# First attention of a two-layer sandwich: projections as three products of rounded parts, v for two heads at once

## The reference

```python
qkv = jnp.einsum('bnd,ed->bne', x, w_qkv)          # x: 4 x 512 x 256, w_qkv: 6144 x 256
q, k, v = to_heads(split(qkv, 3))                  # 16 heads of 128
q, k = rope(q, k)
valid = (j > i - 64) & (j <= i)
scores = where(valid, einsum('bhnd,bhkd->bhnk', q, k) / sqrt(128), -inf)
out = einsum('bhnk,bhkd->bhnd', softmax(scores), v)
y = einsum('bni,di->bnd', out, w_o)
```

## Time and profile before

| what | value |
|---|---|
| median of 3 runs | 3217.12 us |
| lowest and highest | 3216.79 and 3224.24 us |
| the profiled execution's own time | 3226.86 us |
| its span in the profile | 3225.1 us |
| TensorE matmul busy | 2566.4 us, 80% |
| VectorE, ScalarE, GpSimd busy | 52%, 38%, 40% |
| mean granted TensorE clock | 0.908 of full speed |
| first attention, first matmul to last | from 61.7 to 757.2 us of the span |

### The profile page before, as it was taken

The page is one execution under the profiler, slowest core; times in us unless marked ns, Lnnn a source line. Parts: engine busy times, 40 slices in busy tenths (PEclk is TensorE's granted clock), DMA queues, the critical chain, the costliest instruction groups (busy, mean ns, idle before and its releaser), DMA issues. The chain is left out here.

```text
span 3225.1 us, 44443 instructions
## 1 busy us (share of the span) xinstructions
PE 2566.4 (80%) x12088; PEld 1642.3 (51%) x12088; DVE 1680.2 (52%) x5549; ACT 1238.9 (38%) x3462; POOL 1297.1 (40%) x1229
## 2 busy tenths in 40 slices
PE   2999999994699899899989959991385575589993
PEld 1777777773354545545544546651232233266662
DVE  3555555555366366266366353336556456653334
ACT  0333333333355255255255334441154452523331
POOL 0333333332255255155255317883302202106885
PEclk9999999997899999999999959995686887879996
DMA  4000000000100000000000064552000000133554
GB/s 134 11 14 13 13 9 13 13 8 0 75 1 1 1 1 1 1 1 1 2 1 1 1 219 82 86 85 62 21 1 0 0 0 0 62 111 67 87 85 108
DMA packets 72708, 112.21 MB, mean 35 GB/s; under 512 B 11649, under 2 KB 59521, under 8 KB 72129
## 3 DMA queue, kind: packets, MB, share of 16 engines
q0 software_dynamic: 30336, 42.73, 8.3%
q1 hardware_dynamic: 37968, 63.15, 5.7%
q10 hardware_dynamic: 4224, 4.19, 0.4%
HBM read 80.69 MB, written 36.32 MB: 36 GB/s over the span
## 5 line engine op out<-in xcount | busy, mean ns | idle before, releaser
L969 POOL TENSOR_TENSOR b_sm<-b_sm,b_rden 128x128 f32<-128x128 f32 (+3 forms) x512 | 368.0, 721 | 286.0 <-DVE b_rden L937 283.9
L879 ACT ACTIVATE b_sm<-b_sm,b_mn 128x128 f32<-128x128 f32 (+3 forms) x512 | 287.2, 561 | 364.5 <-DVE b_mn L931 364.1
L789 PE MATMUL b_s<-b_k,b_q 128*128 128x128 f32 (+3 forms) x688 | 261.2, 465 | 36.8 <-POOL b_q L956 36.8
L366 POOL TENSOR_TENSOR a_q<-a_prod 128x512 f32<-128x512 f32 x64 | 81.5, 1274 | 485.5 <-DVE a_prod L312 485.5
L931 DVE CUSTOM_DVE_ANT_0 b_sm<-b_s,maskB 128x128 f32<-128x128 f32 (+3 forms) x344 | 167.2, 486 | 160.6 <-issue 158.5
L798 PEld LDWEIGHTS b_t<-ident,b_sm 128*128 128x128 f32 x1280 | 162.2, 141 | 169.6 <-issue 117.4
L798 PE MATMUL b_t<-ident,b_sm 128*128 128x128 f32 x1280 | 225.7, 274 | 11.5 <-DVE b_pt L923 4.9
L1337 POOL DMA_INDIRECT XN<-rows,m_slots x158 | 158.1, 1001 | 95.7 <-DVE m_slots L1499 48.2
L810 PE MATMUL b_o<-b_pt,b_v 128*64 128x512 f32 (+3 forms) x1024 | 191.7, 457 | 3.9 <-DVE b_pt L923 3.9
L789 PEld LDWEIGHTS b_s<-b_k,b_q 128*128 128x128 f32 x688 | 106.2, 194 | 137.5 <-DVE b_mn L931 102.5
L321 DVE CUSTOM_DVE_ANT_0 a_s<-p_s,maskA 128x192 f32<-128x192 f32 (+1 forms) x256 | 71.7, 336 | 200.2 <-issue 200.2
(11 more groups left out here) (278 smaller groups left out, 5812.3 us busy)
## 6 DMA issues: line engine op xcount, KB each, us to landing
WM<-in_m_w_dram SPq DMA_DIRECT2D x4, 3072.0 KB, 15.6
WM<-in_m_w_dram SPq DMA_DIRECT2D x4, 2432.0 KB, 12.9
acc<-in_zeros_dram SPq DMA_DIRECT2D x3, 2176.0 KB, 15.8
a_w<-in_a_w_dram SPq DMA_DIRECT2D x16, 384.0 KB, 3.1
n_part<-acc SPq DMA_DIRECT2D x12, 512.0 KB, 7.8
b_w<-in_b_w_dram SPq DMA_DIRECT2D x1, 3072.0 KB, 10.0
XN<-rows,m_slots POOLq DMA_INDIRECT x158
X<-in_x_dram SPq DMA_DIRECT2D x4, 512.0 KB, 3.8
```

Source lines behind the costliest of these rows:

```text
L789: pe.matmul(p_s[g % 3][:, 0:keys(t)], q_r[:, m % 2, t * P:(t + 1) * P], kp[:, m // B_REP % 2, head, 0:keys(t)], start=True, stop=True).the ...
L879: act.activation(sm[:, g % RING, 0:keys(t)], sm[:, g % RING, 0:keys(t)], ACT.Exp, scale=-1.0, bias=mn[:, g % RING:g % RING + 1], accum_out ...
L969: pool.tensor_tensor(sm[:, s, 0:keys(t)], sm[:, s, 0:keys(t)], rden[:, s:s + 1].to_broadcast([P, keys(t)]), ALU.mult).then_inc(s_pn, 1)
```

## The change

The norm stage n0 writes two arrays in place of one: ScalarE copies the turned rows from PSUM into `HTp[0]`, of type fp32r (rounded, the high part), and VectorE subtracts that from the PSUM value into `HTp[1]` (the low part). The weights of a pair of heads arrive in two pieces: piece a (512 KB: q and k of the first head, v of both heads) and piece b (256 KB: q and k of the second head). ScalarE rounds each piece (`high_a`, `high_b`), GpSimd subtracts (`low_a`, `low_b`). Every projection is then three products, high x high, high x low and low x high, of fp32r operands. v is computed only at u = 0 to 3, for both heads at once, in two halves of the same bank with ScalarE's copy between them. The split of piece a for the next pair stands at the end of step u = 5 on ScalarE and GpSimd, that of piece b at the end of step u = 1; for the first pair both stand at the head of the stage. The last pair is written out as the first is.

```diff
@@ attention0, SyncE
-                load_w(0, 0)
-                load_w(1, 1)
+                load_a(0)
+                load_b(0)
                 load_wo(0)
                 with sp.Fori(1, PAIRS) as i:
-                    sp.wait_ge(s_proj, i * (3 * U) - 3 * BATCH)
-                    load_w(i * 2, 0)
-                    sp.wait_ge(s_proj, i * (3 * U))
-                    load_w(i * 2 + 1, 1)
+                    sp.wait_ge(s_lo_a, i)
+                    load_a(i)
+                    sp.wait_ge(s_lo_b, i)
+                    load_b(i)
@@ attention0, TensorE
+                def three(out, lhs, rhs, k):
+                    for n, (a, b) in enumerate(((0, 0), (0, 1), (1, 0))):
+                        mm = pe.matmul(out, lhs(a), rhs(b), start=(k == 0 and n == 0), stop=(k == KD - 1 and n == 2))
+                    return mm
                 def qk(i, u, j, bank):
+                    w = w_a if u < BATCH else w_b
+                    if j == 0 and b == 0:
+                        pe.wait_ge(s_lo_a if u < BATCH else s_lo_b, i + 1)
                     on(pe, s_prod, 2 * n - 1 + j)
                     for k in range(KD):
-                        mm = pe.matmul(bank[:, :], w[:, slot, k, j, :], c.HT[:, k, b * SEQ:(b + 1) * SEQ],
-                                       start=(k == 0), stop=(k == KD - 1))
+                        mm = three(bank[:, :], lambda a: w[:, a, k, j, :], lambda a: c.HTp[a][:, k, b * SEQ:(b + 1) * SEQ], k)
                     mm.then_inc(s_proj, 1)
                 def v(i, u):
-                    on(pe, s_v, n)
-                    for t in range(TB):
-                        for k in range(KD):
-                            mm = pe.matmul(p_v[:, t * P:(t + 1) * P], c.HT[:, k, b * SEQ + t * P:b * SEQ + (t + 1) * P],
-                                           w[:, slot, k, 2, :], start=(k == 0), stop=(k == KD - 1))
-                    mm.then_inc(s_proj, 1)
+                    for half in range(2):
+                        on(pe, s_v, i * U + 2 * b + half)
+                        for t in range(2):
+                            at = b * SEQ + (2 * half + t) * P
+                            for k in range(KD):
+                                mm = three(p_v[:, t * 2 * P:(t + 1) * 2 * P], lambda a: c.HTp[a][:, k, at:at + P],
+                                           lambda a: w_a[:, a, k, 2:4, :], k)
+                        mm.then_inc(s_proj, 1)
@@ attention0, ScalarE
                 def copy_v(i, u):
-                    act.wait_ge(s_proj, 3 * n + 3)
                     on(act, s_ov, n - 3)
-                    act.activation(v_s[:, u % 4, :, :].rearrange("p t n -> p (t n)"), p_v[:, :], ACT.Copy).then_inc(s_v, 1)
+                    for half in range(2):
+                        act.wait_ge(s_proj, projected(i, u) + 3 + half)
+                        act.activation(v_s[:, :, u, 2 * half:2 * half + 2, :],
+                                       p_v[:, :].rearrange("p (t h n) -> p h t n", t=2, h=2), ACT.Copy).then_inc(s_v, 1)
+                def high_a(i):
+                    act.wait_ge(s_wa, i * 16 + 16)
+                    on(act, s_proj, i * (3 * U) - 2 * BATCH)
+                    act.activation(w_a[:, 0, :, :, :], raw_a[:, :, :, :], ACT.Copy).then_inc(s_hi_a, 1)
@@ attention0, GpSimd
                     if alive(i, u, 0):
                         rope(i, u, 1, k_r)
+                    if u == 5 and more(i):
+                        low_a(i + 1)
+                    if u == 1 and alive(i, u, 0) and (not isinstance(i, int) or i > 0):
+                        low_b(i)
+                def low_a(i):
+                    pool.wait_ge(s_hi_a, i + 1)
+                    pool.tensor_tensor(w_a[:, 1, :, :, :], raw_a[:, :, :, :], w_a[:, 0, :, :, :].bitcast(F32),
+                                       ALU.subtract).then_inc(s_lo_a, 1)
@@ sandwich
-                norm_stage(nc, c, "n0", x_dram=x, outs=((c.HT, None, None),))
-                attention0(nc, c, a_w, a_wo)
+                norm_stage(nc, c, "n0", x_dram=x, outs=((c.HTp, None, None),))
+                attention0(nc, c, a_wa, a_wb, a_wo)
```

More of the change, by code:

```diff
@@ L153, in passes @@
                     step(0, u)
-                with eng.Fori(1, PAIRS) as i:
+                with eng.Fori(1, PAIRS - 1) as i:
                     for u in range(U):
                         step(i, u)
+                for u in range(U):
+                    step(PAIRS - 1, u)
                 for u in range(3):
@@ L168, in out_of, with projected, more @@
                 return (u - 3) % U - BATCH if (u - 3) % U >= BATCH else None
+            def projected(i, u):
+                return i * (3 * U) + (4 * u if u < BATCH else 2 * u + 2 * BATCH)
+            def more(i):
+                return not isinstance(i, int) or i + 1 < PAIRS
             def outs_before(i, u):
@@ L222, in values @@
                         width = P if t == TB - 1 else A_SPAN
-                        mm = pe.matmul(p_o[:, t * P:t * P + width], v_s[:, (u - 2) % 4, t, :], pt[:, t, 0:width],
+                        mm = pe.matmul(p_o[:, t * P:t * P + width], v_s[:, slot, b, t, :], pt[:, t, 0:width],
                                        start=(t == 0), stop=(t == TB - 1), skip_group_check=True)
@@ L248, in step @@
                         turn(i, u)
-                    if alive(i, u, 0):
+                    if alive(i, u, 0) and u < BATCH:
                         v(i, u)
@@ L300, in step @@
                         exp(i, u)
+                    if u == 5 and more(i):
+                        high_a(i + 1)
+                    if u == 1 and alive(i, u, 0) and (not isinstance(i, int) or i > 0):
+                        high_b(i)
+                high_a(0)
+                high_b(0)
                 passes(act, step)
@@ L381, in step, with low_b @@
                         rope(i, u, 1, k_r)
+                    if u == 5 and more(i):
+                        low_a(i + 1)
+                    if u == 1 and alive(i, u, 0) and (not isinstance(i, int) or i > 0):
+                        low_b(i)
[3 more added lines that the diff above has]
+                                       ALU.subtract).then_inc(s_lo_a, 1)
+                def low_b(i):
+                    pool.wait_ge(s_hi_b, i + 1)
+                    pool.tensor_tensor(w_b[:, 1, :, :, :], raw_b[:, :, :, :], w_b[:, 0, :, :, :].bitcast(F32),
+                                       ALU.subtract).then_inc(s_lo_b, 1)
+                low_a(0)
+                low_b(0)
                 pool.wait_ge(s_z, 1)
@@ L424, in norm_stage @@
         has_xn = residual and not final
-        split = any(isinstance(o[0], tuple) for o in outs)
+        split = any(isinstance(o[0], list) for o in outs)
         def sems(used, *names):
@@ L632, in _ @@
                 steps = {}
+                if split:
+                    steps[16] = high_part
                 if store is not None:
@@ L2060, in sandwich @@
                 c.maskA = scope.enter_context(nc.sbuf_tensor("maskA", [P, A_SPAN], F32))
+                c.HTp = [scope.enter_context(nc.sbuf_tensor(f"HT_part{i}", [P, KD, TOKENS], F32R)) for i in range(2)]
                 load("constants_a", ((c.ident[:, :], ident), (c.cosA[:, :], a_cos), (c.sinA[:, :], a_sin),
@@ L2175, in layout @@
     d = {"x": i["L0_attn_x"]}
-    d["a_w"] = i["L0_attn_w_qkv"].reshape(3, A_HEADS, A_HD, KD, P).transpose(1, 4, 3, 0, 2)
+    qkv = i["L0_attn_w_qkv"].reshape(3, A_HEADS // 2, 2, A_HD, KD, P).transpose(1, 5, 4, 2, 0, 3)
+    d["a_wa"] = np.concatenate([qkv[:, :, :, 0, 0:2], qkv[:, :, :, :, 2]], 3)
+    d["a_wb"] = qkv[:, :, :, 1, 0:2]
     d["a_wo"] = i["L0_attn_w_o"].T.reshape(A_HEADS, A_HD, DIM)
```

38 lines of the change are left out of this document (23 added, 15 removed).

## The result

| what | before | after |
|---|---|---|
| median of 4 runs | 3218.68 us | 3272.02 us |
| lowest and highest | 3216.79 and 3224.24 us | 3266.41 and 3272.6 us |
| the profiled execution's own time, and its span | 3226.86 and 3225.1 us | 3266.41 and 3264.6 us |
| first q of the first attention | 61.67 us | 67.10 us |
| last sum into Y | 763.27 us | 812.48 us |

The changed kernel is slower: 1.0159 times the kernel before, 95% interval 1.0141 to 1.0177. In the experiments each ratio is to the kernel before as it ran beside them (medians 3218.68 to 3222.23 us), and differences to the changed kernel are to 3272.02 us.

The account below looks back on a forecast made before the run. Long units were taken as bound by TensorE's matmuls, short ones by a chain through VectorE and GpSimd. Stage +15, start +5.4 and clock +30 made +50 us on the 3217.1 median: 3267 us, range 3228 to 3293.

Parts of the forecast that it names:

- stage without clock: Attention stage: unit-length changes summed over all pairs of heads, +2.8 us a typical pair, together +15 us.
- The start: Before the first q: ScalarE's copy +1.25, larger load +0.6, rounding and subtracting 1.06 + 2.43 + 0.05; sum +5.4 us.
- The stall of v: At u = 0 to 3, TensorE waits 0.86 us between v's halves for ScalarE's copy out of the shared bank.
- Unit 6: Rotary sum of q waits behind GpSimd's subtraction of the next weights: delayed 3.1 us, unit 12.1 us, +2.65.
- Unit 7: Without v, the values wait 1.2 us for ScalarE's copies; unit 10.4 us in place of 11.84, -1.44.
- The product: Projections on TensorE: an fp32r product costs 0.213 us for 512 columns (upper end 0.24), 0.112 for 256.
- the dear product: Rival: products cost 0.24 us for 512 columns and 0.13 for 256, +23 us over the stage, 3290 us; chance 0.12.
- The clock: TensorE's clock falls in short units' gaps at two to four places a pair, 4.3 us a pair, +30 us.
- the holding clock: Rival: no gap is idle enough to lower TensorE's clock, leaving +15 + 5.4, 3237 us; chance 0.14.
- the fast product: Rival: products run quicker than their columns at 2.4 GHz, 0.12 us for 512, about 3204 us; chance 0.06.
- the rounded products do what they say: Rival denying this: fp32r products in the projections cost as much as float32, six times 0.86 for q; chance below 0.01.
- the removed v was off it: At u = 4, 5, v lay off the chain, so removing it saves nothing; only q's 0.43 us counts.

Follow-up runs that it names:

- the kernel of the filled gaps: Changed kernel plus unused float32 matmuls of 512 columns in TensorE's gaps at u = 4 to 6; 3250.62 us, 1.0099 times the kernel before.
- the first experiment: Changed kernel with piece a's split at u = 4, both roundings before the exponentials, subtraction after k's rotary sum; 3250.75 us, 1.0086 times the kernel before.

## Why the prediction was right, step by step

The forecast was 3267 us and the measurement 3272.02, on the side forecast. The steps, with the kernel of the filled gaps as the measurement at the full clock:

| step | predicted | measured, full clock | measured |
|---|---|---|---|
| u = 0 to 2 | 12.73 | 13.18 | 13.18 |
| u = 3 | 9.27 | 9.73 | 9.73 |
| u = 4, 5 | 9.04 | 9.13 | 9.13 |
| u = 6 | 12.1 | 11.99 | 13.08 |
| u = 7 | 10.4 | 10.73 | 11.5 |
| a pair | +2.8 | +5.0 | +6.9 |
| start | +5.4 | | +5.4 |
| stage without clock | +15 | +28 | |
| clock | +30 | | +16 |

- **The start.** Its load, rounding and subtraction were put at 4.14 us beyond today's way to the first product and took 4.13, because each had a row of its own shape or near it. That the sum is 5.4 too is luck: the remaining 1.25, for ScalarE's copy, is smaller than what the same code varies by, and the first q of the eight kernels with this start comes 3.8 to 6.1 us later than in the profiled execution before.
- **The stall of v**, 0.86 predicted, is 0.85. Moving the values into it gives back 0.94, since the first product behind a wait costs 0.10 more, which the sum did not have.
- **Unit 6.** The subtraction was to end at S + 6.9, and the rotary sum behind it starts at 6.86; the delay of 3.1 us for a rotary sum that stands behind foreign work was right, and moving that work removes 2.85.
- **Unit 7.** The values wait 1.11 us for the copies that v used to cover, 1.2 predicted.
- **The product was mis-sized.** "I take 0.213, with 0.24 as the upper end": the records show 0.230 for 512 columns, and 0.119 for 256 in place of 0.112. In a long unit that is 0.20 for q and k, 0.17 for v, and 0.10 for the first product behind the stall: +0.45. Over a pair the full-clock lengths make 2.2 us more than predicted, over the stage 13. The rival of the dear product (0.24 and 0.13) had the right side and twice too much, 0.75 in a long unit where the records give 0.37. For 512 columns my row of 0.24 was nearer than the clock's arithmetic that I preferred to it; for 256 the forecast was nearer. The Trainium skill, "TensorE: Matmul & The Clock Gate", section on the back-to-back issue gap, gives 131 ns for a stream of 512 columns. The trace disagrees by nearly a factor of two for these operands, with 0.230 us.
- **The clock was over-sized.** "I expect a fall at two to four places of each pair, at 1.3 us each": in the loop it falls at one, and costs 1.9 us a pair and not 4.3, so the places were too many and the price of one too low. The earlier trace rows showed a fall after one gap; I carried that over to gaps of 1.1 and 1.6 us, which u = 4 and 5 of the loop survive. The direction was right, and the first experiment and the last pair of the changed kernel show that the fall belongs to the run of short units and not to the long wait.
- **Two slips in the sums.** The terms of a pair and its ends, +17, -1, +1 and -1, make 16 and not 15, and the larger load is 3.8 - 3.1 = 0.7 and not 0.6. Neither moves the forecast beyond the noise.

The two errors cancel: the stage at the full clock was 13 us too cheap and the clock 14 us too dear. That the total is off by 5 us only is luck; the parts are each off by 13 or 14. The rivals: the holding clock (3237) would have been 3250 by the kernel of the filled gaps, since it lacked the dearer product; the dear product (3290) was too dear and kept the whole clock term; the fast product is excluded by the rows; and the rounded products do what they say, 1.39 us for q where float32 takes 1.72. Of the signs named, the clock of the stage came out at 0.96 and not 0.93.

What the prediction named only in passing ("the removed v was off it") turned out to be the heart of the loss: the order costs 10.4 us a pair.

## What to carry to other kernels

Before work is moved between steps, mark for each step whether the engine or a chain bounds it: v of the second head was free where it stood, behind a chain, and cost its full time, and a stall, where it was put, so a change whose products gave back 3.5 us a pair lost 10.4 by its order. Work that belongs to nobody's deadline, such as splitting the next weights, must not stand ahead of a step of the chain on an in-order engine; one unit earlier, and ahead of the exponentials on ScalarE, it lengthened no unit. And a large change is best tested as two, its arithmetic in the old order's terms and its order with the old arithmetic; here the order alone, with each unit given either the output projection or v, wins 1.9 us of a pair, the rounded products in it 5.8, and the two with the shorter start 1.8% of the kernel.

## What the runs showed of the hardware that was not expected

- An fp32r product of 512 columns takes 0.23 us from start to start and one of 256 columns 0.12, above 512 and 256 columns at 2.4 GHz, 0.213 and 0.107. A float32 product takes 0.86 and 0.43, so three fp32r products cost 0.80 to 0.83 of one.
- The starts mislead where fp32r products follow float32 ones: the first is recorded 0.03 us behind its forerunner and the next 0.37 (512 columns) or 0.20 us (256 columns) behind it, whether q has four products or six. Dividing q's 1.52 us by six gives 0.253, which no product costs.
- Behind a wait TensorE's first product takes 0.10 us longer: 0.22 in place of 0.12 (fp32r, 256 columns), 0.32 in place of 0.22 (float32, 256 columns), 0.21 in place of 0.11 (float32, 128 columns).
- The granted clock is not given by the longest gap. In the changed kernel's loop gaps of 1.11 and 1.60 us in two units in a row left it full, and in the first experiment the same gaps in a third brought it to 1.2 GHz; with the transposes first it fell in the second such unit already, and once more in the third.
- Useless matmuls in the gaps made the kernel 21 us faster by the medians, 17 of them by the last sum of the stage (795.43 against 812.48); of that, 1.2 us is a first q that happened to come earlier.
